# Recommender tower on one NeuronCore: the last layer's product on four column groups of the array, and a wait for a product in front of every later gather

## The reference, cut to what matters

```
e = stack([tbl_f[ids[:, f]] for f in range(32)], axis=1)        # (2048, 32, 64)
z = sum(e, axis=-1)                                             # (2048, 32)
outer = einsum('bpd,pde,bpe->bp', e[:, II], kernels, e[:, JJ])  # 496 pairs
h = concatenate([z, outer, dense_ctx], axis=1)                  # (2048, 544)
h = maximum(h @ W_top1 + b_top1, 0)                             # (2048, 512)
h = maximum(h @ W_top2 + b_top2, 0)                             # (2048, 256)
y = h @ W_top3                                                  # (2048, 1)
```

## Time and profile before

| what | value |
|---|---|
| median of 3 runs (lowest to highest) | 820.54 us (820.43 to 821.22) |
| profiled execution, its own time | 820.89 us |
| its span, first to last instruction | 819.1 us |
| TensorE multiplications, busy | 772.8 us, 94% |
| VectorE, busy | 723.0 us, 88% |
| ScalarE, busy | 683.3 us, 83% |
| GpSimd, busy | 607.3 us, 74% |
| granted TensorE clock | 0.994 of full |

### The profile page before, as it was taken

How to read it: one execution, slowest core, us unless ns; L and a number is a source line. 1 busy time by engine, 2 the same in 40 slices (tenths; PEclk the granted TensorE clock), 3 DMA queues, 4 the chain that set the end, 5 groups by cost and what they waited for, 6 DMA issues and landing times.

```text
span 819.1 us, 20179 instructions
## 1 busy us (share of the span) xinstructions
PE 772.8 (94%) x5904; PEld 450.8 (55%) x5904; DVE 723.0 (88%) x684; ACT 683.3 (83%) x5282; POOL 607.3 (74%) x966
## 2 busy tenths in 40 slices
PE   0399989999999999999999999999999999999998
PEld 0245445555555555565555555655555655565556
DVE  0279999989999999989999899989999898998992
ACT  1059897899779997899878997799988998789983
POOL 6776888888888887888868886888868888681000
PEclk9989999999999999999999999999999999999999
DMA  4545111111111111111111111111111111110000
GB/s 135 176 133 166 26 26 25 25 25 26 25 25 26 24 26 22 25 24 26 25 20 25 24 26 21 24 26 25 24 20 24 26 25 24 21 24 7 2 2 1
DMA packets 19966, 28.74 MB, mean 35 GB/s; under 512 B 8968, under 2 KB 9616, under 8 KB 18960
## 3 DMA queue, kind: packets, MB, share of 16 engines
q0 software_dynamic: 16384, 16.81, 10.7%
q1 hardware_dynamic: 3472, 10.63, 3.9%
HBM read 27.40 MB, written 0.01 MB: 33 GB/s over the span
## 4 chain that ended last, share of the span: by engine, by line
PE 80%; POOL 10%; DMA 6%; issue 3%; DVE 1%; ACT 0%; DVEq 0%; POOLq 0%
PE m_ps L645 24%; PE m_ps L629 24%; PE acc L659 13%; POOL gathered L308 9%; PE tr L570 8%; DMA gathered<-in_tbl,idx 5%; PE tr L551 4%; PE tr L584 3%; POOL x_half L291 1%; PE m_ps L570 1%; PE tr L590 1%; PE m_ps L631 1%; PE tr L565 0%; PE m_ps L584 0%; DMA idx<-in_ids 0%
## 5 line engine op out<-in xcount | busy, mean ns | idle before, releaser
L407 ACT ACTIVATE turned_act<-turned_act 128x64 f32<-128x64 f32 x2560 | 611.8, 244 | 3.4 <-DVE turned_act L498 3.3
L308 POOL DMA_INDIRECT gathered<-in_tbl,idx x512 | 489.4, 956 | 99.7 <-issue 75.7
L407 ACT ACTIVATION_READ_ACCUMULATOR turned_act<-turned_act 128x1 f32 x2560 | 488.0, 191 | 0.0
L473 DVE TENSOR_TENSOR prod<-m_ps,x_t 128x1024 f32<-128x1024 f32 x256 | 308.0, 1216 | 25.2 <-PE m_ps L631 24.9
L629 PE MATMUL m_ps<-x_t,k_sb 64*128 64x256 f32 x1024 | 268.8, 389 | 4.8 <-DVE turned_dve L498 2.6
L631 PE MATMUL m_ps<-x_t,k_sb 64*128 64x256 f32 x1024 | 269.2, 389 | 0.0
L645 PE MATMUL m_ps<-k_sb,x_t 64*128 64x512 f32 x1024 | 257.0, 608 | 1.3 <-DVE turned_dve L498 0.7
L629 PEld LDWEIGHTS m_ps<-x_t,k_sb 64*128 64x128 f32 x1024 | 184.2, 188 | 115.1 <-issue 77.5
L498 DVE TENSOR_TENSOR turned_act<-m_ps,gathered 128x1024 f32<-128x1024 f32 x160 | 192.7, 1217 | 14.0 <-PE m_ps L645 6.0
L631 PEld LDWEIGHTS m_ps<-x_t,k_sb 64*128 64x128 f32 x1024 | 184.0, 188 | 0.0
L291 POOL TENSOR_TENSOR x_half<-gathered 128x32 f32<-128x32 f32 x448 | 117.2, 262 | 34.7 <-DVE z_nat L457 25.7
(11 more groups left out here) (36 smaller groups left out, 159.3 us busy)
## 6 DMA issues: line engine op xcount, KB each, us to landing
gathered<-in_tbl,idx POOLq DMA_INDIRECT x512, 2.4
k_sb<-in_kmat SPq DMA_DIRECT2D x7, 1024.0 KB, 4.8
w_sb<-in_w SPq DMA_DIRECT2D x1, 1280.0 KB, 9.5
k_sb<-in_kmat SPq DMA_DIRECT2D x2, 256.0 KB, 3.1
k_sb<-in_kmat SPq DMA_DIRECT2D x1, 512.0 KB, 4.6
w_sb<-in_w SPq DMA_DIRECT2D x1, 512.0 KB, 11.1
idx<-in_ids SPq DMA_DIRECT2D x1, 256.0 KB, 2.7
z_sb<-in_dense_t SPq DMA_DIRECT2D x8, 16.0 KB, 1.7
```

Source lines behind the costliest of these rows:

```text
L308: nc.gpsimd.indirect_dma_start(out=gathered[:, t, G % GR, f * D:(f + 1) * D], out_offset=None, in_=tables[2 * (STAGES - 1 - a) + f], in_of ...
L407: last = nc.scalar.activation(row, row, ACT.Copy, accum_out=z_turned[:, q % 2, t, 16 * c + n:16 * c + n + 1])
L473: nc.vector.tensor_tensor(prod[:, r % PR, :, :].rearrange("p u (e n) -> p u e n", e=2), m_ps[:, p % MR, :, :].rearrange("p u (e n) -> p u ...
```

## The change

Three things are edited. `layer3` cuts its 256 data columns into four pieces of 64 and gives each its own group of 32 array columns, with the result on partitions 0, 32, 64 and 96 of `tr`; so it has 8 multiplications of 64 columns in place of 2 of 256. ScalarE's copy takes 64 columns of all 128 partitions (of which four carry results) in place of 256 columns of one, and the store takes four partitions with 64 numbers each. And GpSimd, from gather 64 on, waits ahead of gather k until k - 40 products are done.

```diff
+LEAD = 40
+YC = 4
+YN = QB // YC
@@
-        y_sb = sb("y_sb", [1, QB])
+        y_sb = sb("y_sb", [P, YN])
@@ GpSimd, ahead of each gather
+                if k >= FIRST_K:
+                    pool.wait_ge(prod_ready, k - LEAD)
                 nc.gpsimd.indirect_dma_start(
@@ SyncE, the store of each part (the last one likewise)
-                    sp.dma_start(out[:, (q - 1) * QB:q * QB], y_sb[:]).then_inc(y_stored, 16)
+                    sp.dma_start(out[:, (q - 1) * QB:q * QB].rearrange("o (g n) -> (o g) n", n=YN), y_sb[0:P:32, :]).then_inc(y_stored, 16)
@@ ScalarE, keep_y and the last copy
-                nc.scalar.activation(y_sb[:], tr[0:1, 0, :], ACT.Copy).then_inc(tr_kept, 1)
+                nc.scalar.activation(y_sb[:], tr[:, 0, 0:YN], ACT.Copy).then_inc(tr_kept, 1)
@@ TensorE
-            def layer3(to):
+            def layer3():
                 for c in range(H2 // P):
-                    last = nc.tensor.matmul(to, w3_sb[:, c:c + 1], h2_sb[:, c, :],
-                                            start=(c == 0), stop=(c == H2 // P - 1))
+                    for g in range(YC):
+                        last = nc.tensor.matmul(tr[32 * g:32 * g + 1, 0, 0:YN], w3_sb[:, c:c + 1], h2_sb[:, c, g * YN:(g + 1) * YN],
+                                                start=(c == 0), stop=(c == H2 // P - 1))
                 return last
```

## The result

| | median | lowest to highest | runs |
|---|---|---|---|
| before | 820.52 us | 820.1 to 821.22 | 6 |
| after | 816.22 us | 815.87 to 816.82 | 6 |

The ratio is 0.9948, 95% interval 0.9935 to 0.9961: 4.3 us faster, where the prediction said 815.6 us and 4.9 us. The profiled execution took 816.19 us, its span is 814.4 us (819.1 before) at a granted clock of 0.991.

What follows compares the result with a forecast made beforehand. GpSimd was taken to bound the kernel up to 148 us, then TensorE. Savings of 4.2 + 0.6 + 0.17 = 5.0 us gave 815.9 from the profiled execution, 815.5 from the median; forecast 815.6 us, range 814.7 to 818.2.

Steps and rivals of the forecast that it cites:

- What bounds the kernel: GpSimd sets the time up to 148 us, TensorE until about 790 us; at the end every step counts whole.
- the hand-over: At 148.00 us TensorE begins to turn gathered pieces, released by GpSimd's halving; forecast to stay at 148.0 us.
- Layer 3 in the stream: Layer 3 behind 148 us, on four column groups side by side: 0.60 us saved each of 7 times, 4.2 us.
- rival 1: Layer 3's weight loads lie in the open: 0.29 us saved a time, 2.5 us in all, 818.0 us; chance 0.12.
- The end: Last part: layer 3 saves 0.60 us, ScalarE's copy 0.17, the store changes nothing (bounds 0 to +0.5 us).
- A fulfilled wait: Ahead of GpSimd's gathers before 148 us: an already fulfilled wait costs under 0.01 us, taken as 0.
- rivals 2 and 4: Fulfilled waits cost GpSimd 0.05 us each, 817.2 us, chance 0.08; or 0.16 us each, 828 us, chance 0.06.
- Held gathers: From part 3 on GpSimd's gathers wait for products, yet TensorE comes 6.7 us after the halving in part 5.
- The sign of being wrong: A part of 95 us or longer, or a row of TensorE waiting for `x_half` behind 150 us.
- rival 3: Layer 3's groups do not go side by side: only 0.17 us saved at the end, 820.4 us; chance 0.06.
- This part of the change is worth 0 us.: The wait ahead of gathers, from part 3 on: nobody waits for held gathers and even supply gains nothing, 0 us.

Runs made afterwards that it cites:

- `cut_in_one_group`: Changed kernel with layer 3's four pieces all in one column group, copy and store as before: 821.15 us, ratio 1.0007 to the kernel before.
- `groups_only`: Changed kernel without the wait ahead of the gathers: 1230.73 us, ratio 0.9916 on a chip where the kernel before takes 1238.13 us.

## Why the prediction was right, point by point

**What bounds the kernel.** Right on this kind of chip: the hand-over stands at 147.94, and from there TensorE is busy throughout.

**Layer 3 in the stream.** Right: 0.60 us a time were forecast; seven layers 3 gave 0.62 to 0.63 us each from the hand-over on, together 4.39 us (4.2 forecast, 0.19 short). The bunches are 0.055 us apart (0.05 forecast), the groups start within 7 ns of each other, and the even step follows after 0.34 us (0.35). VectorE, which stood idle for 0.71 us behind layer 3, does so for 0.09 (0.11 forecast). `cut_in_one_group`, with the same pieces one after another, loses all of it.

**Weight loads (rival 1).** Wrong, as I had held. The Trainium skill, page "TensorE: Matmul & The Clock Gate", section on packing small matmuls, has loads overlap a running multiplication only when they go to other rows; its part on the mechanism also lets them run ahead into a background weight buffer, which the prediction left out. This kernel's runs speak against it twice: 16 loads of 84 ns to the same rows fit into 0.22 us with four groups, and into 0.87 us in one group. With 64 data columns the spacing of multiplications follows the columns alone.

**The end.** The step that failed in size. Forecast: 0.60 for layer 3, 0.17 for the copy, nothing for the store; measured: 0.59 and 0.15, less 0.45 of the store, 0.3 us in all. I had bounded the store at +0.5 us and taken the lower end, by a load of 16 pieces that landed in 1.7 us. But that row has the time to landing without one for fewer pieces beside it, so it could not tell what the pieces add. With the 0.45 us the sum would have been 4.5 us and 816.4 us from the profiled execution; it took 816.19. The terms of the profiled pair add up to its 4.7 us (4.39 in the stream, 0.28 at the end, 0.06 ahead of the hand-over, where nothing was meant to change). The layers in the stream gave 0.2 us more than forecast and the end 0.5 less, so the misses partly cancelled; that the forecast of the median came within 0.6 us owes a little to it.

**A fulfilled wait (rivals 2 and 4).** It costs nothing that shows: in the changed kernel 30 gathers up to 146.65 us come in 41.95 us, 1.398 us each, where they came at 1.396.

```profile
104.70 0.96 POOL L313 DMA_INDIRECT gathered<-in_tbl,idx  x1 [0.16 <-issue]
...
146.65 0.96 POOL L313 DMA_INDIRECT gathered<-in_tbl,idx  x1 [0.16 <-issue]
```

**Held gathers.** Right: GpSimd waits from part 3 on, no multiplication of TensorE does, and the pieces for stages 8 and 9 of part 5 are halved at 519.77 and turned at 526.26, 6.5 us later (6.7 forecast). The sign of being wrong, a row of TensorE that waits for `x_half` behind 150 us, was too wide: weight loads have such rows before and after.

**Groups not side by side (rival 3).** Wrong; it is what `cut_in_one_group` looks like, 95.23 us a part.

**"This part of the change is worth 0 us."** Right for the chip on which the pair was measured, and shown by `cut_in_one_group` on another of its kind. Wrong as a sentence on the kernel: on two other chips the wait alone takes 22 to 23% off, and no trace of the kernel before was kept from one of these. The prediction had no case for it, and no row of the trace of before could have given one, because on that chip 8 and more gathers back to back leave TensorE's rate where it is. `groups_only` itself was not run on a chip of the 820 us kind.

**Still open** is why the engines starve. The gathers take 957 ns on both kinds of chip. In places TensorE's records come in ticks of about 0.7 us, half the distance of two gathers (the four starts from 523.59 to 525.75 above), as if something let them through once per half gather. The Trainium skill, page "Runtime: NRT & Kernel Launch", section "Instruction fetch mechanics", has each engine's instructions refilled in blocks of 256 through a DMA queue of its own. A queue held up by the gathers' descriptors would fit with idle engines, but engines that ran dry of a whole block would stop for long and then run, not tick. In rows of eight or more gathers I count 8 packets of the instruction queues in some 250 us of `groups_only` and 14 per 100 us on the other kind of chip; which is cause and which effect was not shown. The gathers' own packets are not held up: 32 of them end per gather in the rows of eight and more, as on the other kind of chip. A second rival is the recording itself: all executions here are profiled ones, and semaphore records are lost just on the chips where the engines starve, and there just beside indirect DMAs. Against it: they are lost at positions 1 to 3 as well, where TensorE still goes at 7.6. No run without recording is on record, so it is not shown that such a chip is as slow without the profiler. Nor do I know what sets the two kinds of chip apart.

## What to carry to other kernels

Where TensorE is busy without a gap, a product with one weight column costs by its data columns, so cutting them over four column groups is worth three quarters of it each time it stands in the stream (0.62 of 0.84 us here); at the program's end count the store's pieces too, because a store from several partitions takes back more than half of what the shorter copy and product gave (0.45 of 0.74 us). And it is worth trying to pace an engine that may run far ahead with indirect DMAs by its consumer, even where that measures as nothing: here it was free on one kind of chip and a quarter of the time on another, as long as the lead was not too short (34 in place of 40 gave part of it back). A change of such pacing is only measured when it has run on more than one chip.

## What the runs showed of the hardware that I had not expected

- Chips of one type run the same kernel, recorded, in 820 us and in 1238 to 1272 us. In the parts whose indirect DMAs give way to ordinary ones the difference vanishes, to 94.58 us a part, though the ordinary ones follow each other every 0.76 us and the indirect ones every 1.40.
- On such chips TensorE's rate falls from 7.6 records per us to 4.5 from the fourth indirect DMA of a row on and to about 2 from the eighth on; VectorE and ScalarE fall with it, and so does TensorE's granted clock (0.84 over such a run, 0.96 with the wait). The traces of these chips lack up to two thirds of the semaphore updates that gathers make on landing.
- A store from two or four partitions at the end holds SyncE's queue for 0.48 and 0.50 us, one from a single partition for 0.24 to 0.26. From the issue's start to SyncE's going on it is 1.51 and 1.56 us in place of 1.11.
- Four copies of 1 x 64 from PSUM by VectorE take 0.96 us, 0.21 to 0.23 each; one copy by ScalarE of 64 columns of all 128 partitions takes 0.22.
